# First layer: the products of the queries with the key-value matrices, moved out of the loop over units to its end, around the experts and beside the folding of the second layer's weights

## What is computed

```python
xn = layernorm(x)
q, k, v = split(xn @ W); q = elu(q) + 1; k = elu(k) + 1      # layer 1, linear attention
KV = einsum('bld,blh->bhd', k, v);  k_sum = k.sum(axis=1)     # one 256x256 matrix for each row
Z = 1.0 / (einsum('bld,bd->bl', q, k_sum) + EPS)
s = einsum('bld,bhd,bl->blh', q, KV, Z)                       # "values"
e = argmax(xn @ gate_w.T)                                     # one of 8 experts for each token
g = silu(square(relu(xn @ wg[e])) * (xn @ wu[e]) @ wd[e])
x = x + s * g
xn = layernorm(x)                                             # layer 2: causal softmax attention in
s = block_attention(xn, W_qkv, blocks of 128) @ W_out.T + b_out
x = x + s * silu(layernorm(xn) * ln_g + ln_b)                # its 16 heads take 8 // 16 = 0 tokens each
```

## Time and profile before

| | us |
|---|---|
| median of three runs | 572.27 (571.80 to 572.69) |
| the profiled execution: its own time | 571.23 |
| its span | 569.6 |
| PE busy | 511.5 (90%) |
| DVE busy | 467.0 (82%) |
| ACT busy | 401.4 (70%) |
| POOL busy | 359.0 (63%) |

### The profile page before, as it was taken

The page is one execution under the profiler, slowest core; times in us unless marked ns, Lnnn a source line. Parts: engine busy times, 40 slices in busy tenths (PEclk is TensorE's granted clock), DMA queues, the critical chain, the costliest instruction groups (busy, mean ns, idle before and its releaser), DMA issues. The chain is left out here.

```text
span 569.6 us, 13050 instructions
## 1 busy us (share of the span) xinstructions
PE 511.5 (90%) x3666; PEld 470.0 (83%) x3667; DVE 467.0 (82%) x1458; ACT 401.4 (70%) x907; POOL 359.0 (63%) x431
## 2 busy tenths in 40 slices
PE   0888999999999999748799996779999999999995
PEld 0887999999999999738789985567887888888884
DVE  4799887888888877675678783859999999999985
ACT  3776888787877877226577763448787788788884
POOL 4478888797878787613122203788878888887400
PEclk9999999999999999779999997789999999999999
DMA  8812223232222311127767655246556656656311
GB/s 229 225 37 75 75 75 92 72 98 74 74 74 74 96 41 52 64 76 240 234 219 248 206 176 184 64 103 136 142 115 132 138 119 130 146 112 143 78 56 55
DMA packets 59548, 68.07 MB, mean 119 GB/s; under 512 B 11880, under 2 KB 53744, under 8 KB 59504
## 3 DMA queue, kind: packets, MB, share of 16 engines
q1 hardware_dynamic: 44016, 38.69, 22.0%
q0 software_dynamic: 15488, 28.85, 21.5%
HBM read 40.25 MB, written 27.26 MB: 119 GB/s over the span
## 5 line engine op out<-in xcount | busy, mean ns | idle before, releaser
L1613 POOL DMA_INDIRECT moe<-expert_rows,gather_u x64 | 68.3, 1067 | 40.7 <-DVE gather_u L1456 22.1
L810 POOL DMA_INDIRECT sorted_rows<-xn,row_u x64 | 64.0, 999 | 18.1 <-issue 14.4
L1275 PE MATMUL q_ps<-xt,wqk 128*128 128x256 f32 x256 | 63.2, 391 | 0.7 <-ACT xt L1381 0.7
L891 POOL DMA_DIRECT2D xg<-sorted_rows x36 | 19.7, 549 | 65.0 <-issue 45.0
L1297 PE MATMUL v_ps<-wvo,xt 128*128 128x256 f32 x256 | 60.5, 379 | 0.0
L794 POOL TENSOR_TENSOR xn<-xn 128x512 fp32r<-128x512 f32 x32 | 41.4, 1294 | 25.0 <-ACT xn L429 23.4
L1275 PEld LDWEIGHTS q_ps<-xt,wqk 128*128 128x128 f32 x256 | 50.3, 197 | 8.3 <-ACT xt L1381 1.0
L1401 ACT ACTIVATE xn2nd<-res,shift,rstd 128x256 f32<-128x256 f32 (+1 forms) x64 | 34.9, 593 | 27.9 <-POOL shift L1633 27.9
L1297 PEld LDWEIGHTS v_ps<-wvo,xt 128*128 128x128 f32 x256 | 46.3, 190 | 5.0
L1631 POOL TENSOR_TENSOR rstd<-var_eps,neg_half 128x4 f32<-128x4 f32 x32 | 38.2, 1195 | 17.7 <-DVE var_eps L1498 9.6
L117 PE MATMUL m_ps<-k,xn 128*128 128x256 f32 x128 | 37.5, 293 | 7.6 <-DVE k L573 5.6
(11 more groups left out here) (225 smaller groups left out, 1866.2 us busy)
## 6 DMA issues: line engine op xcount, KB each, us to landing
expert_rows<-y SPq DMA_DIRECT2D x36, 256.0 KB, 2.9
xa<-in_L_attn_x SPq DMA_DIRECT2D x32, 256.0 KB, 2.8
out_rows<-att SPq DMA_DIRECT2D x32, 256.0 KB, 2.7
res<-in_L_attn_x POOLq DMA_DIRECT2D x28, 256.0 KB
xg<-sorted_rows SPq DMA_DIRECT2D x36, 128.0 KB, 2.4
xg<-sorted_rows POOLq DMA_DIRECT2D x36, 128.0 KB, 2.9
wdn<-in_L_ffn_wd SPq DMA_DIRECT2D x2, 512.0 KB
sorted_rows<-res SPq DMA_DIRECT2D x8, 128.0 KB, 5.8
```

What stands on the lines that cost most here:

```text
L810: nc.gpsimd.indirect_dma_start(out=z.sorted_dram.ap(), out_offset=bass.IndirectOffsetOnAxis(ap=row_u[:, i // CU, k:k + 1], axis=0), in_=xn ...
L1275: m = nc.tensor.matmul(q_ps[:, j, :], wqk[:, k, j * P:(j + 1) * P], xt[:, i % 2, k, :], start=(j == 0 and k == 0), stop=(k == KD - 1), ski ...
L1613: nc.gpsimd.indirect_dma_start(out=moe[:, i % SLOTS, t, :], out_offset=None, in_=z.expert_dram.ap(), in_offset=bass.IndirectOffsetOnAxis(a ...
```

## The change

The loop no longer multiplies queries with the key-value matrices. `exp_q` and `fill_q` write the queries into the unit's own result rows in `z.res` (they are "parked"), the matrices of up to 6 rows are kept, and the 32 products of a unit ("v0" to "v31") are done later, each as round (ACT), split (POOL or DVE), product (PE), divisors (DVE), scaling into `z.res` (ACT), through 4 query slots. Seven are placed early in steps 25 to 31 and four more late in steps 28 to 31; v11 to v20 follow the last step, with the tables between them on DVE; v21 and v22 stand at the start of the experts, v23 to v25 behind their last pair, and v26 to v31 at the start of the second layer, between turning and folding. The diff, cut to its core, shows in this order the new functions, the tables of numbers, the step of PE, of ACT, of DVE and of POOL in the first layer, PE's start and ACT's end of the experts, and DVE's start of the second layer.

```diff
+def by_pool(v):
+    return v < 6 or 15 <= v <= 18 or 23 <= v <= 25
...
+def round_query(nc, act, z, v):
+    act.wait_ge(z.q_full, v + 1)
+    if v >= Q_SLOTS:
+        act.wait_ge(z.v_ready, v - Q_SLOTS + 1)
...
+def query_values(nc, pe, z, v, banks):
+    row = v * z.UT * P // z.L
+    pe.wait_ge(z.kv_split, row + 1)
+    pe.wait_ge(z.q_split_pool if by_pool(v) else z.q_split, sum(by_pool(u) == by_pool(v) for u in range(v + 1)))
...
+        EARLY = {25: 0, 26: 1, 27: 2, 28: 3, 29: 5, 30: 7, 31: 9}
+        LATE = {28: 4, 29: 6, 30: 8, 31: 10}
+        TAIL = range(11, 21)
...
             def step(n, i, r):
                 turn(n + 1, at(i, 1))
...
+                values(of_step(EARLY, n), 0)
+                kv(n, i, r)
                 keys(n, i, r)
-                if not there(n):
-                    count(n, i, r)
-
-                kv(n, i, r)
-                before = lambda: sums(n - 1, at(i, -1), r if i else r - 1)
-                if not row_closed(n, i, r):
-                    before()
-                values(n - V_LAG, at(i, -V_LAG), r if i >= V_LAG else r - 1)
-                if row_closed(n, i, r):
-                    before()
+                sums(n - 1, at(i, -1), r if i else r - 1)
+                values(of_step(LATE, n), 0)
...
+                rows(of_step(LATE, n - 1))
                 exp_q(n, i)
-                scale_rows(n - V_LAG - 1, at(i, -V_LAG - 1))
+                rows(of_step(EARLY, n))
                 round_kv(n, i, r)
                 exp_keys(n, i)
                 if not begin:
                     norm_apply(n + 2, at(i, 2))
-                round_q(n, i)
                 round_xn(n, i)
                 round_keys(n, i)
+                round_next(of_step(EARLY, n + 1))
+                round_next(of_step(LATE, n + 1))
...
+                divisors(of_step(LATE, n - 1))
                 split_keys(n - 1, at(i, -1))
-                invert_divisors(*late)
...
                 fill_q(n, i)
                 find_moments(*ahead)
+                divisors(of_step(EARLY, n))
...
                 keep_pick(n, i, r)
...
+                split_next(of_step(EARLY, n + 1))
+                split_next(of_step(LATE, n + 1))
+                if isinstance(n, int) and n in (UNITS - 3, UNITS - 2):
+                    centre_experts(n - UNITS + 3)
...
                 placed(n - SCATTER_LAG, at(i, -SCATTER_LAG), r if i >= SCATTER_LAG else r - 1)
-                split_q(n - 1, at(i, -1))
+                split_xn(n, i)
                 scatter(n - SCATTER_LAG, at(i, -SCATTER_LAG))
-                split_xn(n, i)
+                split_next(of_step(EARLY, n + 1))
+                split_next(of_step(LATE, n + 1))
...
+            for v in START:
+                query_values(nc, pe, z, v, value_banks[v])
             pe.wait_ge(g["wdn_split"], 1)
             four_pairs(0, True, False)
...
+            for v in END:
+                round_query(nc, act, z, v + 3)
+                scale_values(nc, act, z, v, value_banks[v])
...
+            invert_sums(nc, dve, z, VALUES[0], value_banks(VALUES[0]))
+            split_query(nc, dve, z, VALUES[3])
+            invert_sums(nc, dve, z, VALUES[1], value_banks(VALUES[1]))
+            step(-6, TURN - 6, 0)
+            split_query(nc, dve, z, VALUES[4])
...
+            for v in VALUES[3:]:
+                invert_sums(nc, dve, z, v, value_banks(v))
+            run(dve, -4, step, UNITS + 1)
```

More of the change, by code:

```diff
@@ L21 @@
 MASKED = 3.0e38
+Q_SLOTS = 4
+KV_ROWS = 6
 class Names:
@@ new lines, in invert_sums, with scale_values @@
+def invert_sums(nc, dve, z, v, banks):
+    dve.wait_ge(z.v_ready, v + 1)
+    nc.vector.tensor_scalar(z.zsum[:, v % Q_SLOTS], banks[:, :, z.D], Z_EPS, 2.0, ALU.add, ALU.mult).then_inc(z.zsum_ready, 1)
+    dve.wait_ge(z.zsum_ready, v + 1)
+    nc.vector.reciprocal(z.zinv[:, v % Q_SLOTS], z.zsum[:, v % Q_SLOTS]).then_inc(z.zinv_ready, 1)
+def scale_values(nc, act, z, v, banks):
+    act.wait_ge(z.zinv_ready, v + 1)
+    for t in range(z.UT):
+        nc.scalar.activation(z.res[:, z.UT * v + t, :], banks[:, t, 0:z.D], ACT.Copy,
+                             scale=z.zinv[:, v % Q_SLOTS, t:t + 1]).then_inc(z.rows_ready, 1)
@@ L407, in _ @@
             t.then_inc(g["gate_turned"], 1)
-            run(pe, -1, step, UNITS - 1 + V_LAG)
+            run(pe, -1, step, UNITS - 1)
+            count(UNITS, 0, 0)
+            sums(UNITS - 1, SLOTS - 1, UNITS // SLOTS - 1)
+            values(TAIL[0], 0)
+            pe.wait_ge(g["k_read"], UNITS)
+            pe.wait_ge(g["base_moved"], CHUNKS)
+            values(TAIL[1], 2)
+            pe.wait_ge(z.q_full, UNITS)
+            pe.wait_ge(g["t_split"], UNITS)
+            values(TAIL[2], 2)
+            kv(UNITS + 1, 1, UNITS // SLOTS)
+            for v in TAIL[3:]:
+                values(v, 2)
         @block.scalar
@@ L470, in round_kv, with rows, round_next @@
             def round_kv(n, i, r):
-                closed = row_closed(n, i, r)
-                if closed:
-                    act.wait_ge(g["kv_ready"], closed[0] + 1)
-                    nc.scalar.activation(kv2[:, closed[1], 0], m_ps[:, :, 0:NV], ACT.Copy).then_inc(g["kv_rounded"], 1)
-            def scale_rows(n, i):
-                if there(n):
-                    act.wait_ge(g["zinv_ready"], n + 1)
-                    if isinstance(n, int) and n == UNITS - 1:
-                        act.wait_ge(g["zeros_stored"], 16 * E)
-                    for t in range(UT):
-                        nc.scalar.activation(z.res[:, bass.ds(UT * n + t, 1), :], v_bank(n)[:, t, 0:D].unsqueeze(1), ACT.Copy,
-                                             scale=zinv[:, i, t:t + 1]).then_inc(g["rows_ready"], 1)
+                b = row_closed(n, i, r)
+                if b is not None:
+                    act.wait_ge(g["kv_ready"], b + 1)
+                    if isinstance(b, int) and b >= KV_ROWS:
+                        act.wait_ge(z.v_ready, (b - KV_ROWS + 1) * ROW)
+                    nc.scalar.activation(kv_row(b, 0), m_ps[:, :, 0:NV].unsqueeze(1), ACT.Copy).then_inc(g["kv_rounded"], 1)
+            def rows(v):
+                if v is not None:
+                    scale_values(nc, act, z, v, tail_banks(v))
+            def round_next(v):
+                if v is not None:
+                    round_query(nc, act, z, v)
             def round_weights(which):
@@ L1006, in dn @@
                 def dn(i):
+                    if first and i == 0:
+                        pe.wait_ge(z.rows_ready, z.UT * (START[1] + 1))
                     down(n + i, i, e[i], not first or i >= 2)
```

398 lines of the change are left out of this document (245 added, 153 removed).

## The result

The changed kernel takes 648.46 us (median of 4 runs, 645.76 to 650.72), the kernel before 572.06; the ratio is 1.1332, with a 95% interval of 1.1285 to 1.1379. I had forecast 608, from 583 to 622: the direction was right, the size was not. The profiled execution took 650.72 us with a span of 649.0, 79.4 more than before.

The account below looks back on a forecast made before the run. It took PE as the loop's bound before, and a cycle through ACT's norm and POOL's split and transfers after. Terms 2.4 + 20.2 + 5.9 + 2.0 − 2.3 + 4.1 + 4 = +36.3 on 571.23 gave 608 us, range 583 to 622.

Parts of the forecast that it names:

- What bounds the kernel: First layer's loop: PE bound before; afterwards a cycle through ACT's norm and POOL's split and transfers, 6.5 us a step.
- the clock's term: Steps from 24 on: PE's waits cause one or two falls to half clock at some 2.7 us each, +4 us.
- The tail's term: From the last fill of the keys to the block's end: five more products, less the centring, 25.3 us, +2.0.
- The loop: Steps 4 to 24: ordinary steps 6.5 us, row-closing steps 8.2, so 138.5 us against 136.12, +2.4.
- The early steps: Steps 24 to 29: PE waits for POOL's splits of early products, 55.7 us against 35.5, +20.2.
- The first rival: Clock falls in every early step: 13 us instead of 4, total 617 us; chance 0.13.
- The stretch to the last fill: Steps 29 to 31: two products a step and their hand-overs, 18.8 us against 12.9, +5.9.
- The experts' start: Tiles arrive in the tail already, so gate and up begin 4.4 us into the block instead of 6.7, −2.3.
- The experts' end and the second layer: v23 to v25 hold the barrier 2.4 us longer; third unit's `scale_rows` moves by some 7.3; together +4.1.
- the second: Rival for steps 24 to 29: only POOL's queue grows, +6.9, with no clock term; total 591 us, chance 0.11.
- the third: Rival for the loop: DVE bounds it, 123.5 us for twenty steps, −12.7; total 569 us, chance 0.06.
- fourth: Rival for the loop: PE stays the bound at 5.4 us a step, −25.3; total 557 us, chance 0.09.

Follow-up runs that it names:

- e1: Changed kernel with POOL's two transfers back ahead of the split of the normed rows: 602.54 us, ratio 1.0547.
- e11: Kernel before the change with one edit, POOL's transfers behind the split of the normed rows: 585.20 us, ratio 1.0251.
- e4: Changed kernel with POOL's half of the first four pairs' loads issued at the start of the experts again: 640.65 us, ratio 1.1215.
- e3: Changed kernel with query products computed twice before step 24 and three times in steps 24 to 31, same result, to keep PE busy: 635.93 us.
- e10: e6 with v0 to v2 behind the sums, v3 ahead of step 28's keys and v4 to v10 moved to the tail's front: 599.83 us.
- e12: e6 with v0 to v2 behind the sums and the splits of v15 to v18 by DVE instead of POOL: 590.95 us, ratio 1.0343.
- e2: Changed kernel with the splits of the parked queries v0 to v5 by DVE instead of POOL: 622.53 us, ratio 1.0898.
- e6: Changed kernel with the edits of e1 and e2 together: 599.34 us, ratio 1.0487.
- e5: Changed kernel with kv behind keys in PE's row-closing steps, as before the change: 640.81 us, ratio 1.1213.

## Why the prediction was wrong

**What bounds the kernel: right.** That the loop would gain nothing, because POOL's order closes a cycle through ACT's norm, is shown from both sides: e1 takes the transfers out of the cycle of the changed kernel (−24 us in the loop, of which some 5 are the clock), e11 puts them into that of the old one (+11).

**Where the 43 us are.** The profiled executions differ by 79.4 us, and my terms add up to 36.3. Of the 43.1 that are missing, 15 are the clock (19 against 4), 10 the tail, 5 the loop apart from the clock, 5 the experts' end with the second layer, 3 each the stretch to the last fill and the experts' start, and 2 the early steps. The step that failed is the clock's term: I priced one or two falls at 2.7 us, +4, and the traces show one in each of the five early steps, three in the loop and more up to the last fill, about 19. The tail's term is the next: +2.0, and +12.0 measured.

**The loop, +2.4 forecast, +12.1 in the profile.** The ordinary steps take 6.8, not 6.5. 0.26 of it is the first transfer, which takes 1.30 us (193.59 above) where I had 1.04 from the earlier trace rows. The row-closing steps take 8.3 at the full clock (I had 8.2) and up to 10.6 at the half. The clock fell in three of the five in the changed kernel (granted 0.68, 0.68 and 0.81, in steps of 10.5, 10.6 and 9.0 us) and in two in e4, whose loop is the same (0.81 and 0.81, 8.8 and 9.0 us). There the stretch took 144.1, so this term is +8 to +12.

**The early steps, +20.2 forecast, +34.1.** Wait and chain were right: with the clock held up (e3) the five steps take 58.0, and I had 55.7. The rest of the miss here, too, is the clock.

**The clock, +4 forecast, about +19.** This is the main error. I took its price from two waits of 3 us, of which one was followed by a fall, and counted only the five long waits, and of these one or two falls; all five steps have one. And the sentence that the experts' stretch shows no slow passes holds behind 273.02 only: at the block's start, behind the wait of 7.30, the first eight products of gate and up take 1.53 where eight at the full clock take 1.06. Table by stretch of the kernel before:

```profile
249.70:256.00 6.30, 1.53 (x6) 1.19 (x7) 5.03 (x5) 0.60 (x2) 2.26 (x4) 0.57 0.39 129
262.00:273.00 11.00, 7.08 (x57) 6.43 (x55) 6.97 (x16) 5.81 (x14) 2.19 (x4) 1.00 0.89 293
```

The falls came with waits of 1.8 us in the loop as well. Timeline of PE in a row-closing step of the changed kernel:

```profile
102.81 0.66 PE L371 MATMUL tq_ps<-ident,xn 128*128 128x128 f32 x4 [1.84 <-ACT xn L498]
...
104.25 0.37 PE L128 MATMUL tq_ps<-xt,wq 128*128 128x256 f32 x1
104.42 0.42 PE L126 MATMUL tq_ps<-xt,wq 128*128 128x256 f32 x1
104.64 0.41 PE L127 MATMUL tq_ps<-xt,wq 128*128 128x256 f32 x1
```

The passes go from 0.12 to 0.21 apart in the middle of a product, 1.4 us behind the wait. The waits of PE in steps 4 to 24 (us in total, times, longest), of the changed kernel and then of e1, whose clock stayed at 1.00:

```profile
PE tq_ps L371 <- ACT xn L498: 24.4, 17, 1.9
PE m_ps L126 <- DVE m L720: 3.9, 5, 1.3
```

```profile
PE m_ps L126 <- DVE m L721: 6.6, 5, 2.4
PE tq_ps L372 <- ACT xn L499: 4.8, 14, 0.4
```

In e1 the five waits for `m` are 1.3, 1.0, 1.0, 2.4 and 1.0 us, one in each four steps, and no fall followed any of them; 1.5 to 1.9 in nearly every ordinary step was followed by a fall in some row-closing steps. The price by rows: 5.0 in the loop (the three steps with a fall against 8.35, the last row-closing one, at the full clock), 11.6 in steps 24 to 29 and 2.3 to the last fill (both e3 against the changed kernel), 19 in all; e3's median, with its slower start, shows 12.5. The first rival (every early step at half clock, +13) had this right: the page of the Trainium skill that I weighed in the prediction, "TensorE: Matmul & The Clock Gate", section "HAM oscillation — how this bites in real kernels", says that a recurring wait can throttle the engine again in each round, and this trace agrees (granted clock 0.76 over the five steps, and below 1.00 in each). It would have moved my sum to 617, and still not to 648.

**The stretch to the last fill, +5.9 forecast, +11.3.** 2.3 is the clock (e3: 21.9); the rest is a chain that I had summed 3 us too short. e10 prices it: 9.8 us for the four products that stand in this stretch (v6 to v9), 2.4 each.

**The tail, +2.0 forecast, +12.0** (+9.0 in e1 to e3). Three things were missing. POOL's transfers moved into the tail hold the barrier for 4.3 us (e4: 4.77 to 0.49), and POOL's splits hold those transfers (e12: −5 to −7.5). A product in the tail costs 2.5 (e10), where my 15.4 of ACT for eleven makes it 1.4. And 3 us are DVE's wait whose cause stays open. I had followed the transfers only to the tiles' arrival, not to the end of the block that issues them.

**The experts' start, −2.3 forecast, +0.8.** The tiles were there, but v21 and the first passes of v22 ran at the half clock behind PE's idle time at the barrier:

```profile
320.86 1.94 PE L1052 MATMUL t_ps<-ident,four 128*128 128x128 f32 x8 [6.92 <-issue]
...
322.46 0.56 PE L126 MATMUL ht_ps<-kv,qs 128*128 128x258 f32 x1
...
325.18 0.42 PE L126 MATMUL y_ps<-kv,qs 128*128 128x258 f32 x1
...
327.05 1.05 PE L1061 MATMUL gu_ps<-wgu,xgt 128*128 x8
```

v21 takes 2.7 us instead of 1.44, and gate and up begin 7.6 us into the block, where they began at 6.7.

**The experts' end and the second layer, +4.1 forecast, +8.8.** From gate and up to the second layer the experts take 4.7 longer (I had 2.4 of it; what the rest is no run shows), and the second layer 4.0. The third unit's `scale_rows` (442.03, 18.3 us into its block; before 12.6) moved by 5.7; I had 7.3.

```profile
442.03 0.69 DVE L1627 TENSOR_TENSOR res<-four,res 128x512 f32<-128x512 f32 x1
```

The other rivals did not come: the second (early steps at 42.4) is near what e2 and e6 reach, but by an edit, and the third and fourth needed the transfers outside the cycle. With them outside, in e1, the loop takes 124.5, near the third's price (123.5) and far from the fourth's (110.9).

## What to carry to other kernels

Taking work off the engine that is busy 90% of the time gained nothing here, because the order of another engine's queue closed a cycle just below it: write the cycle out, with every instruction that stands between the two hand-overs, transfers too, before you count the busy share. When a change makes PE wait in nearly every step, as here for 1.5 to 1.9 us, price the whole step at both clocks; the cheap test is to give PE useless work, which made this kernel 12.5 us faster. A load that is moved ahead of a barrier has a price there: four of POOL's held it for 4.3 us.

## What the runs showed of the hardware

TensorE's clock fell to its lower level (1.2 GHz, passes 0.21 us apart) in a stretch in which PE never waited longer than 1.9 us, but waited for 1.5 to 1.9 us in nearly every ordinary step (mean granted clock 0.94 in the loop); it stayed up in the loop of e1, with waits of 0.3 to 0.4 us in most steps and five of 1.0 to 2.4, and in that of e11, with waits of 0.9 us and less but for one. In which of the row-closing steps it falls differs between executions: the same loop took 148.2 us in the changed kernel's profile and 144.1 in e4's. DVE's wait for a barrier was 4.3 us longer when GpSimd's last transfers had been issued shortly ahead of it, and DVE's first instruction behind it came 6.46 or 6.47 us after the start of the last of them in eleven traces. An indirect transfer's issue took 1.30 us on GpSimd for the first of a pair in three of four steps of the changed loop and of e11's, and 1.03 or 1.04 in the loops of the kernel before and of e1, with few exceptions; the second took 0.96. Why is not shown. In the changed kernel's tail DVE waited 4.03 us, at a point where v12, which it was to divide, had left PE 5 us before (292.07). Waits of 2.7 to 4.1 us stand at the same point, the sums of the tail's second product, in e5 to e10, and none in e1 to e4 and e12. With it the tail takes 34.0 to 35.6 us, without it 32.3 or 32.4 (e1 to e3; e10 and e12 have other tails). Its cause stays open:

```profile
291.79 0.28 PE L128 MATMUL k_ps<-kv,qs 128*128 128x258 f32 x1
...
297.04 0.16 DVE L174 TENSOR_SCALAR zsum<-k_ps 128x2 f32<-128x2 f32 x1 [4.03 <-remote]
```
